# A three-layer decoder kernel: x loaded first, weight work on GpSimd, and the second LayerNorm inside the self-attention loop

## What is computed

```python
def reference(x, ctx, ...):                       # x, ctx: (128, 64, 128) float32
    x = x + attn(layernorm(x), Wq, Wk, Wv)        # 16 heads of 8, one K and one V for all heads
    x = x + xattn(layernorm(x), ctx, ...)         # two LSTM layers and attention over ctx, 64 steps in sequence
    x = x + ffn(layernorm(x), router, W1, b1, W2, b2)   # top 1 of 8 experts, 512 wide
    return x
```

## Time and profile before

| | us |
|---|---|
| median of three runs | 1586.23 |
| profiled execution | 1586.78 |
| its span | 1585.1 |
| PE busy | 1332.6 (84%) |
| DVE busy | 1126.3 (71%) |
| ACT busy | 761.3 (48%) |
| POOL busy | 430.9 (27%) |

### The profile page before, as it was taken

How to read it: one execution, slowest core, us unless ns; L and a number is a source line. 1 busy time by engine, 2 the same in 40 slices (tenths; PEclk the granted TensorE clock), 3 DMA queues, 4 the chain that set the end, 5 groups by cost and what they waited for, 6 DMA issues and landing times. The chain is left out here.

```text
span 1585.1 us, 83126 instructions
## 1 busy us (share of the span) xinstructions
PE 1332.6 (84%) x34523; PEld 1212.1 (76%) x34523; DVE 1126.3 (71%) x4638; ACT 761.3 (48%) x2223; POOL 430.9 (27%) x1193
## 2 busy tenths in 40 slices
PE   1627777777756999999999999999999999929997
PEld 1416666666635899999999999999999999829996
DVE  4878888888884676777776677677667677636664
ACT  1427777777732444444444444444444444415553
POOL 0000000000001133333333333333333333324444
PEclk9769999999967999999999999999999999959999
DMA  7000000000034000000000000000000000022332
GB/s 252 1 1 3 3 4 2 3 3 3 3 107 142 9 19 17 19 19 18 19 19 20 16 19 18 20 20 19 18 18 17 20 19 20 11 84 77 95 94 60
DMA packets 42253, 52.60 MB, mean 33 GB/s; under 512 B 5754, under 2 KB 33788, under 8 KB 41752
## 3 DMA queue, kind: packets, MB, share of 16 engines
q1 hardware_dynamic: 35232, 32.77, 7.2%
q0 software_dynamic: 5344, 12.66, 2.3%
q10 hardware_dynamic: 1304, 1.86, 0.3%
HBM read 28.31 MB, written 19.42 MB: 30 GB/s over the span
## 5 line engine op out<-in xcount | busy, mean ns | idle before, releaser
L447 POOL TENSOR_TENSOR X<-X,yv 128x128 f32<-128x128 f32 x64 | 29.4, 459 | 411.4 <-DVE yv L657 411.4
L1049 PE MATMUL sc_ab<-h_a,KH 128*128 128x48 f16 (+2 forms) x4096 | 123.2, 183 | 2.2 <-DVE h_a L1386 2.2
L1049 PE MATMUL sc_ab<-h_b,KH 128*128 128x48 f16 (+2 forms) x4096 | 123.3, 182 | 0.5 <-issue 0.5
L1099 PEld LDWEIGHTS mx_ab<-pmv_b,VH 128*128 128x128 f16 x4096 | 107.1, 96 | 16.2 <-DVE pmv_b L1429 16.2
L976 PE MATMUL z_a<-h_a,WL 128*128 128x64 f16 x2304 | 112.1, 193 | 7.4 <-DVE h_a L1378 1.9
L1099 PE MATMUL mx_ab<-pmv_b,VH 128*128 128x16 f16 x4096 | 113.0, 169 | 5.2 <-DVE pmv_b L1429 0.4
L976 PE MATMUL z_b<-h_b,WL 128*128 128x64 f16 x2304 | 112.0, 193 | 5.7 <-DVE h_b L1378 0.4
L1122 ACT ACTIVATE gt_a<-z_a,sc 128x256 f32<-128x256 f32 x128 | 60.8, 475 | 115.4 <-PE z_a L976 115.4
L1049 PEld LDWEIGHTS sc_ab<-h_a,KH 128*128 128x128 f16 x4096 | 113.2, 96 | 2.3 <-DVE h_a L1386 2.3
L1049 PEld LDWEIGHTS sc_ab<-h_b,KH 128*128 128x128 f16 x4096 | 113.3, 96 | 0.8 <-issue 0.7
L1099 PE MATMUL mx_ab<-pmv_a,VH 128*128 128x16 f16 x4096 | 112.3, 169 | 0.4 <-DVE pmv_a L1429 0.2
(11 more groups left out here) (294 smaller groups left out, 3734.6 us busy)
## 6 DMA issues: line engine op xcount, KB each, us to landing
xr<-sorted_x SPq DMA_DIRECT2D x71, 129.0 KB, 2.1
XT<-in_ctxT SPq DMA_DIRECT2D x1, 4096.0 KB, 13.4
x_scratch<-X SPq DMA_DIRECT2D x1, 4096.0 KB, 16.0
x1r<-x_scratch SPq DMA_DIRECT2D x64, 64.0 KB, 1.8
X<-in_w SPq DMA_DIRECT2D x1, 2048.0 KB, 9.1
sorted_x<-zt SPq DMA_DIRECT2D x12, 129.0 KB, 3.3
out<-ys,xr POOLq DMA_INDIRECT x71
sorted_x<-TOK,slot POOLq DMA_INDIRECT x64, 2.9
```

Of the source, the lines that this page charges most:

```text
L447: nc.gpsimd.tensor_tensor(xrow, xrow, yv[:, 1 - u, :, :].rearrange("p (g a) d -> p a g d", g=4), ALU.add).then_inc(g_x1, 1)
L1049: mm = nc.tensor.matmul(A.S[:, WIDE * n:WIDE * n + streamed(n)], KH[:, k, pair * P:(pair + 1) * P], A.h[1][:, 2 * n:2 * n + streamed(n) // ...
L1099: mm = nc.tensor.matmul(A.M[:, WIDE * n:WIDE * (n + 1)], VH[:, k, pair, :], A.pm[:, 2 * n:2 * n + WIDE // 2, :].rearrange("p b k -> p (b k)"),
```

## The change

- The loads of x (eight) come first on SP's queue, then those of ctx (four). The small weights move to ACT's queue, behind the biases.
- The statistics of the first LayerNorm move from block 2 to the head of DVE's program in block 1, eight pairs for each load of x; the square root goes to ACT before its scalings. The maximum of ctx is taken in four parts and one more reduce.
- The bias splitting moves from DVE to POOL, both layers at once. The low halves of WL move to POOL too, into steps 2 to 11 of the self-attention loop (weight_rest, two blocks a step, two instructions each).
- Block 3 goes. Its work is done in the self-attention loop, which runs to i = 70: DVE aggregates pair i-2, POOL makes the reciprocal roots of four pairs at once (x1_rstd, seven instructions, every fourth step) and normalizes pair i-6 (x1n), PE transposes it at the end of its step into bank 1 of psT, and DVE writes both halves of XT for pair i-7. PE's transposes of pr wait before bank 1 until that has been read. X is stored in eight parts by SP within the loop.

```diff
+        early_ctx = ExitStack()
+
+        def sbe(name, shape, dt=F32):
+            return early_ctx.enter_context(nc.sbuf_tensor(name, shape, dt))
+        wl32 = sbe("wl32", [P, 20 * P])
+        wlt = sbe("wlt", [P, P])
+        st6 = sbe("st6", [P, NPAIR, 6])
+        mv = sbe("mv", [P, NPAIR, 2])
+        sd = sbe("sd", [P, NPAIR])
+        rs = sbe("rs", [P, NPAIR])
+        XCH, CCH = 8, 4
...
             with nc.Block() as block:
                 @block.sync
                 def _(sync):
-                    sync.dma_start(CT, ctxT).then_inc(s_ctx, 16)
-                    sync.dma_start(xwq_sb[:, :], xwq).then_inc(s_wo, 16)
...
-                    sync.dma_start(Xp, x.rearrange("(n two) t d -> (two t) n d", two=2)).then_inc(s_x, 16)
-                    sync.wait_ge(s_x, 16)
+                    xw = x.rearrange("(n two) t d -> (two t) n d", two=2)
+                    nx, ncx = NPAIR // XCH, B * T // CCH
+                    for k in range(XCH):
+                        sync.dma_start(Xp[:, k * nx:(k + 1) * nx, :], xw[:, k * nx:(k + 1) * nx, :]).then_inc(s_x[k], 16)
+                    for k in range(CCH):
+                        sync.dma_start(CT[:, k * ncx:(k + 1) * ncx], ctxT[:, k * ncx:(k + 1) * ncx]).then_inc(s_ctx[k], 16)
 
...
@@ -186,6 +198,14 @@
...
+                    act.dma_start(xwq_sb[:, :], xwq).then_inc(s_wo, 16)
...
+                    act.dma_start(bo_sb[:, :], bo.rearrange("(p a) -> p a", a=1)).then_inc(s_wo, 16)
+                    act.wait_ge(v_st, 2 * NPAIR + 1)
+                    nc.scalar.activation(sd[:, :], sd[:, :], ACT.Sqrt).then_inc(a_sd, 1)
                     act.wait_ge(v_scale, 1)
...
+                    pool.wait_ge(s_b, 16 * 12)
...
+                    bias_step(pool.tensor_tensor(bw[:, :, :], bb[:, 0::2, :], bb[:, 1::2, :], ALU.add))
+                    pool.wait_ge(v_scale, 1)
+                    for layer in range(2):
+                        bias_step(pool.tensor_scalar(bw[:, layer, :], bw[:, layer, :], sc[:, layer:layer + 1], S,
+                                                     ALU.mult, ALU.mult))
+                    bias_step(pool.tensor_scalar(bw[:, :, 2 * P:3 * P], bw[:, :, 2 * P:3 * P], 2.0, None, ALU.mult))
+                    for k in range(3):
+                        bias_step(pool.tensor_copy(bhi[:, :, :], bw[:, :, :]))
+                        r = slice(32 * k, 32 * k + 1)
+                        bias_step(pool.tensor_copy(BL[r, :, :], bhi[r, :, :]))
+                        if k < 2:
+                            bias_step(pool.tensor_tensor(bw[:, :, :], bw[:, :, :], bhi[:, :, :], ALU.subtract))
+
...
                     for c in range(16):
+                        if c % (16 // CCH) == 0:
+                            pe.wait_ge(s_ctx[c // (16 // CCH)], 16)
                         if c >= 2:
...
-
+                    for n in range(NPAIR):
+                        if n % (NPAIR // XCH) == 0:
+                            dve.wait_ge(s_x[n // (NPAIR // XCH)], 16)
+                        nc.vector.bn_stats(st6[:, n, :], Xp[:, n, :]).then_inc(v_st, 1)
+                    for n in range(NPAIR):
+                        dve.wait_ge(v_st, n + 1)
+                        nc.vector.bn_aggr(mv[:, n, :], st6[:, n, :]).then_inc(v_st, 1)
+                    dve.wait_ge(v_st, 2 * NPAIR)
+                    nc.vector.tensor_scalar(sd[:, :], mv[:, :, 1], EPS, None, ALU.add).then_inc(v_st, 1)
...
-                    dve.wait_ge(s_ctx, 16)
-                    nc.vector.tensor_reduce(mx[:, 4:5], CT, AX.X, ALU.max,
-                                            apply_absolute_value=True).then_inc(v_mx, 1)
+                    for k in range(CCH):
+                        dve.wait_ge(s_ctx[k], 16)
+                        nc.vector.tensor_reduce(mxc[:, k:k + 1], CT[:, k * (B * T // CCH):(k + 1) * (B * T // CCH)], AX.X, ALU.max,
+                                                apply_absolute_value=True).then_inc(v_mx, 1)
+                    dve.wait_ge(v_mx, 7 + CCH)
+                    nc.vector.tensor_reduce(mx[:, 4:5], mxc[:, :], AX.X, ALU.max).then_inc(v_mx, 1)
...
-                    dve.wait_ge(s_const, 9)
+                    dve.wait_ge(a_sd, 1)
+                    nc.vector.reciprocal(rs[:, :], sd[:, :]).then_inc(v_rs, 1)
...
-                    for layer in range(2):
-                        step2(nc.vector.tensor_tensor(bw[:, :], bb[:, 2 * layer, :], bb[:, 2 * layer + 1, :], ALU.add))
-                        step2(nc.vector.tensor_scalar(bw[:, :], bw[:, :], sc[:, layer:layer + 1], S, ALU.mult, ALU.mult))
-                        step2(nc.vector.tensor_scalar(bw[:, 2 * P:3 * P], bw[:, 2 * P:3 * P], 2.0, None, ALU.mult))
...
-                            step2(nc.vector.tensor_copy(bhi[:, :], bw[:, :]))
-                            if k == 0:
-                                step2(nc.vector.tensor_scalar(BL[:, layer, :], bhi[:, :], rowm[:, 0:1], None, ALU.mult))
-                            else:
-                                step2(nc.vector.scalar_tensor_tensor(BL[:, layer, :], bhi[:, :], rowm[:, k:k + 1],
-                                                                     BL[:, layer, :], ALU.mult, ALU.add))
-                            step2(nc.vector.tensor_tensor(bw[:, :], bw[:, :], bhi[:, :], ALU.subtract))
-
-                    for blk in range(20):
-                        col = (S0 if blk < 12 else S1) + (8 if blk % 4 == 2 else 0)
-                        dve.wait_ge(a_w, blk + 1)
-                        nc.vector.scalar_tensor_tensor(WL[:, blk, 1, :], wl32[:, blk * P:(blk + 1) * P],
-                                                       sc[:, col:col + 1], WL[:, blk, 0, :],
-                                                       ALU.mult, ALU.subtract).then_inc(v_w, 1)
...
             def run_steps(eng, step):
-                for i in range(-3, NPAIR + 1):
+                for i in range(-3, NPAIR + 7):
                     step(i, i % 2)
 
             with nc.Block() as block:
+                @block.sync
+                def _(sync):
+                    x1w = x1_dram.rearrange("(n two) t d -> (two t) n d", two=2)
+                    for n in range(0, NPAIR, 8):
+                        sync.wait_ge(g_x1, n + 8)
+                        sync.dma_start(x1w[:, n:n + 8, :], Xp[:, n:n + 8, :]).then_inc(s_x1, 16)
+                    sync.wait_ge(s_x1, 16 * NPAIR // 8)
+
                 @block.gpsimd
                 def _(pool):
+                    def weight_rest(blk):
+                        col = (S0 if blk < 12 else S1) + (8 if blk % 4 == 2 else 0)
+                        if blk > 0:
+                            pool.wait_ge(g_wl, 2 * blk)
+                        pool.tensor_scalar(wlt[:, :], wl32[:, blk * P:(blk + 1) * P], sc[:, col:col + 1], None,
+                                           ALU.mult).then_inc(g_wl, 1)
+                        pool.wait_ge(g_wl, 2 * blk + 1)
+                        pool.tensor_tensor(WL[:, blk, 1, :], wlt[:, :], WL[:, blk, 0, :], ALU.subtract).then_inc(g_wl, 1)
...
+                    def x1_rstd(q):
+
+                        k = 6 * q
+                        pool.wait_ge(v_ag2, 4 * q + 4)
+                        pool.tensor_scalar(ve4[:, :], x1_mv[:, 4 * q:4 * q + 4, 1], EPS, None, ALU.add).then_inc(g_r2, 1)
+                        pool.wait_ge(g_r2, k + 1)
+                        pool.tensor_tensor(yr4[:, :], ve4[:, :], mh4[:, :], ALU.pow).then_inc(g_r2, 1)
...
+                        pool.tensor_tensor(x1_rs[:, 4 * q:4 * q + 4], yr4[:, :], yu4[:, :], ALU.mult).then_inc(g_rs2, 1)
+
                     def step(i, u):
+                        if 2 <= i < 12:
+                            weight_rest(2 * i - 4)
+                            weight_rest(2 * i - 3)
+                        if has(i - 6):
+                            n = i - 6
+                            pool.wait_ge(g_rs2, n // 4 + 1)
+                            wait(pool, p_x1t, n - 1)
+                            pool.tensor_scalar(x1n[:, n % 2, :], Xp[:, n, :], x1_mv[:, n, 0:1], x1_rs[:, n:n + 1],
+                                               ALU.subtract, ALU.mult).then_inc(g_x1n, 1)
                         if has(i - 1):
                             n = i - 1
                             pool.wait_ge(v_y, n + 1)
                             xrow = X[:, bass.ds(n * D, D)].rearrange("p (a g d) -> p a g d", a=QA, g=4)
                             nc.gpsimd.tensor_tensor(xrow, xrow, yv[:, 1 - u, :, :].rearrange("p (g a) d -> p a g d", g=4),
                                                     ALU.add).then_inc(g_x1, 1)
+                        if has(i - 2) and i % 4 == 1:
+                            x1_rstd((i - 2) // 4)
+
                     run_steps(pool, step)
...
+                                if hp == 4 and has(i - 7):
+                                    pe.wait_ge(v_x1l, i - 6)
                                 mm = nc.tensor.transpose(psT[:, hp // 4, (hp % 4) * P:(hp % 4 + 1) * P],
...
```

(43 more changed lines are left out.)

143 lines of the change are left out of this document (52 added, 91 removed).

## The result

The changed kernel takes 1545.46 us (median of four runs, 1545.32 to 1549.22), the kernel before 1586.03 beside it: a ratio of 0.975, 95% interval 0.9734 to 0.9767. The forecast was 1544.0 with a range of 1530 to 1562. The profiled execution took 1545.54 us, its span is 1543.8.

What follows compares the result with a forecast made beforehand. Limits differed by stage: transfers first in the prologue, DVE alone before the first xn, DVE busy 286 of 338.5 us in the attention steps. 1586.8 - 2.7 - 17.5 - 23.6 + 6.4 + 2.1 - 7.6 = 1543.9, forecast 1544, range 1530 to 1562.

Steps and rivals of the forecast that it cites:

- The scale at 45.0, block 2 at 82.6, gain 2.7: Prologue: with x first the scale comes 10.8 us later, yet the block ends at 82.6, gaining 2.7 us.
- a clock that rises sooner: Prologue: if PE's shorter pause keeps the clock up, some 3 us more gain, not in the sum.
- First xn, 17.5: Start of self-attention: 4.3 us left of 21.8 before the first xn, as the LayerNorm statistics leave; gain 17.5 us.
- The old stage, 23.6: Old LayerNorm stage behind the loop: it goes, leaving a short tail to 455.3; gain 23.6 us (22 to 25).
- The step, 0.10 us: Attention loop: DVE's two halves and bn_aggr cost 0.10 us a step, 6.4 us over 64 steps.
- a sign of being wrong: Wrong if a step exceeds 5.2 us, POOL or DVE's own halves release the reduce, or the recurrence changes length.
- POOL late, 2.1: Attention loop: POOL, overfull in steps with WL work and rstd, delays X at DVE's bn_stats; 2.1 us lost (0 to 5).
- Six of nine dips go, 7.6: Attention loop: six of nine falls of PE's clock to 1.2 GHz vanish as the transpose fills its pause; gain 7.6 us.
- The dips stay: Rival, attention loop: the falls of PE's clock remain, 1551.5 us; chance 0.25.
- Nothing hides: Rival, attention loop: DVE pays 0.48 us a step instead of 0.10, 1566 us; chance 0.12.
- DVE and POOL block each other: Rival, attention loop: xn waits for a POOL instruction in 26 steps, 9 us, 1553 us; chance 0.05.
- x first costs more than it gives: Rival, prologue: x lands at 27, scale at 50, block ends at 87.6, 1549 us; chance 0.04.

Runs made afterwards that it cites:

- late_half: Changed kernel with DVE's high half of XT moved from ahead of xh's low half to behind it; 1566.03 us, ratio 0.9866 to the kernel before.
- fill_t1: Changed kernel with one idle transpose in PE's pause of each attention step; ratio 0.9712 to the kernel before, on a slower chip.
- fill_t2: Changed kernel with two idle transposes in PE's pause of each attention step; ratio 0.9703 to the kernel before, on a slower chip.
- fill_t4: Changed kernel with four idle float32 transposes in PE's pause of each attention step; 1534.32 us, ratio 0.9671 to the kernel before.
- ctx_first: Changed kernel with ctx loaded ahead of x and the statistics of x done behind the scale; 1530.45 us, ratio 0.965 to the kernel before.
- spread_wl: Changed kernel with one WL block a step in steps 2 to 21, not two in 2 to 11; 1541.01 us, ratio 0.9717 to the kernel before.

## Why the prediction was right, and which step was wrong

The time was hit within 1.5 us. Five of the six terms of its sum came out within 2 us of what was forecast; the sixth, the dips, failed. By its steps:

- **The scale at 45.0, block 2 at 82.6, gain 2.7.** Measured 45.4, 82.24 and 3.1. The last bn_stats ends at 24.6, 24.1 forecast. PE's third chunk came at 53.31, 0.6 later than forecast; 0.5 of that is WO's low half, held by POOL (see the next section). The bias work on POOL, bounded at 20 us, took 13.5 (45.59 to 59.06) and is hidden. The bound did not follow from its row: the eleven instructions behind the scale go over some 9,500 columns, which at 0.46 per 128 is 34 us, more than the cover of 30. It held because a long instruction is cheaper by the column, 2.12 us for the subtraction of 1024 columns and 1.04 for the cast. What I left open as a bound, a clock that rises sooner, did happen, but smaller: PE's pause was 4.33 us, the clock was low from 54.1 to 57.5 (before, to 61.0), and from the third chunk to the block's end it took 28.9 us instead of 29.9, 1 us and not 3.
- **First xn, 17.5.** Measured 17.5, at 4.23 us behind the block's start.
- **The old stage, 23.6.** Measured 23.9. Two terms were off and nearly cancelled in a tail of 9.7 us: x1n is 0.80 and not 0.45 (priced like an add), and the four single pairs came 1.25 apart, not 1.35.
- **The step, 0.10 us.** Measured 0.07, 4.4 us over 63 intervals. late_half shows why: the wait of 0.34 for ACT hides the high half. The argument from the gaps in the earlier trace rows was right to 0.03 us. The reduce does start straight behind DVE's own low half now, which I had named as a sign of being wrong; it costs only 0.02.
- **POOL late, 2.1.** Measured 1.0 to 1.1, in two steps. DVE waits 1.8 us for X in three places, but the steps grow by less. The chain of roots was priced right (2.9, 3.1 forecast) and x1n too low (0.80, not 0.45).
- **Six of nine dips go, 7.6.** This step failed. The changed kernel had ten, and seven the second time, against nine and ten in the two kernels with the old loop. The mechanism, that the filling of PE's pause before xn's transpose decides, is right in its direction: fill_t1, fill_t2 and fill_t4 have 3, 1 and 0. What was wrong was its size. I said "only just at the edge" from nine hits in 60, and took 0.23 us for two thirds of the way. The five executions with a pause of 1.17 and even steps had 10, 7, 6, 7 and 6, 7.2 on average: x1's transpose removes about two. The next one, down to 1.06, removes all of those in the last 47 steps.
- **What took its place.** The dips' 7.6 did not come, and the tenth dip cost about 1 more. The forecast held because the step was 2.0 cheaper than priced (6.4 against 4.4), POOL 1.0, the prologue and the tail 0.7, and because the recurrence and experts, which aren't touched, were 2.8 us shorter. The last is luck, and I had named it as a sign of being wrong: without it the time would have been some 1548, still in the range. Their length lies between 1100.9 and 1105.75 in the kernels of the first two chips, with the old and the new loop alike, and no run tells why.
- **Rivals.** "The dips stay" was the true case, at 1551.5, with a chance of 0.25; measured by its own mechanism it came out 6 us lower for the reasons just given. "Nothing hides" is refuted by late_half. "DVE and POOL block each other" is hardly there: xn is 0.43 to 0.47 us in three steps crowded by POOL (0.33 otherwise), but 0.335 on average over the 64, though POOL is at work beside it in 21 of them. "x first costs more than it gives" was wrong as an outcome, yet ctx_first shows that the order costs 12 us against another one that was open.

## DVE held by POOL

The prediction had this rival for the loop and not for the prologue. In ctx_first the 8x8 instruction of dg (L312) takes 1.08 us, from 23.37 to 24.45; POOL's addition of the biases runs from 22.08 to 24.42. Before the change, with POOL idle, and in the whole change, with POOL idle at that point too, it is 0.22:

```profile
31.30 0.22 DVE L270 TENSOR_SCALAR dg<-ident,mxr 8x8 f32<-8x8 f32 x1
```

```profile
42.53 0.22 DVE L321 TENSOR_SCALAR dg<-ident,mxr 8x8 f32<-8x8 f32 x1
...
46.57 0.58 DVE L359 TENSOR_SCALAR pmask<-par 64x128 f32<-64x128 f32 x1
...
51.72 0.88 DVE L363 SCALAR_TENSOR_TENSOR WO<-wo_sb,sc,WO 128x128 f16<-128x128 f32 x1 [4.57 <-ACT WO L214]
```

DVE's instruction ends as POOL's does, 0.86 us late, on the path that sets the scale. pmask (0.22 before, 0.58) and WO's low half (0.35 before, 0.88 here) overlap POOL's chain of biases in the same way. POOL of the kernel after:

```profile
45.59 1.49 POOL L254 TENSOR_SCALAR bw<-bw,sc 128x512 f32<-128x512 f32 x2 [31.07 <-DVE sc L343]
...
50.33 2.12 POOL L262 TENSOR_TENSOR bw<-bw,bhi 128x1024 f32<-128x1024 f32 x1
```

pmask ends at 47.15 and POOL's scaling at 47.08, WO's low half at 52.60 and POOL's subtraction at 52.45. dg and pmask are tensor_scalars, WO's low half a form with two inputs in SBUF. The Trainium skill, "SBUF — State Buffer", section Who interferes with whom, says that a DVE instruction in a mode that uses both port pairs, which tensor_scalar can enter, and one with two SBUF inputs beside a GpSimd instruction that reads SBUF, contend for a port pair that is locked as a whole, the later one waiting for the whole of the earlier. These three agree. Not every tensor_scalar is held, though. DVE and POOL of spread_wl:

```profile
140.26 0.33 DVE L713 TENSOR_SCALAR xn<-X,mv,rs 128x128 f32<-128x128 f32 x1
```

```profile
139.69 0.80 POOL L522 TENSOR_SCALAR x1n<-X,x_mv,x_rs 128x128 f32<-128x128 f32 x1
```

Here xn, for which the prediction feared the rule, runs its usual 0.33 us wholly inside POOL's x1n. Where it was longer in the changed kernel it was so by 0.10 to 0.14 us; at 141.12 it ends 0.28 before POOL's x1n beside it. What sets it apart from dg and pmask no run tests. Where one input is PSUM the loop shows nothing of it either: in the steps crowded by POOL, too, each half from psT takes 0.28 us (at 135.73 and 136.12, with WL's work running beside).

## What the runs showed of the hardware that was not expected

- PE's granted clock falls to half, 1.2 GHz, in a loop whose longest pause is 1.17 to 1.41 us: 6 to 10 times in some 310 us, for 3.4 us each, at 1.1 to 1.26 us of time apiece. With a pause of 0.74 or 0.82 us it doesn't, and in the even steps of fill_t1, at 1.06 us, it doesn't either.
- Idle transposes cost nothing there (a step stays 4.99 us with up to four) and give 11.1 us.
- The first 14 us, mostly x in 512 B pieces, moved 263 GB/s, the next 14, mostly ctx in longer ones, 349. The Trainium skill, "DMA: Bandwidth & Descriptors", section Specifications, names 512 B as enough for full line rate. That is again not borne out.
- POOL: a tensor_scalar with two per-partition operands on 128x128 float32 takes 0.80 us (x1n), an add 0.46, a power on 128x4 1.04.

## What to carry to other kernels

A piece of work put ahead of a wait that is already there cost nothing here, behind it it cost all of its length: read the waits of 0.3 us in a step and place the new instructions by them. Before crediting a change with a better clock, measure it: put idle work into the pause, which prices the whole of it in one run. Do not read the number of falls from one execution: the same kernel had ten and seven. And when a load or a statistic is moved to the head of a queue, ask what else that queue feeds; here the scale needed ctx, and filling the later gaps with the statistics gave what the new order gave and 12 us more.
